# Routed slots with transposed gate and up products, expert weights copied ahead by ScalarE, tables built in the last round, and fillers issued by SyncE and GpSimd

## The reference

```python
logits = hidden @ router_w.T                        # 16 experts
top_vals, top_idx = jax.lax.top_k(logits, 1)
scores = sigmoid(top value at top_idx, -inf elsewhere)
routed_in = hidden[None] * scores.T[:, :, None]
gate, up = split(einsum('nth,nhf->ntf', routed_in, gate_up_proj))   # f = 128 each
routed_out = einsum('ntf,nfh->nth', up * silu(gate), down_proj)
shared = silu(hidden @ shared_gate_w.T) * (hidden @ shared_up_w.T) @ shared_down_w.T
return shared + routed_out.sum(axis=0)
```

## Time and profile before

| | |
|---|---|
| median of 3 runs | 595.18 us (593.46 to 595.81) |
| the profiled execution's own time | 601.01 us |
| its span, first to last instruction | 599.2 us |
| mean granted TensorE clock | 0.941 |
| busy: PE, PEld, DVE, ACT, POOL | 515.9, 408.7, 402.7, 303.2, 348.1 us |
| the 80 stores L1146 | 78.8 us busy, GpSimd idle before them 109.9 us |
| HBM traffic | 21.15 MB read, 17.47 MB written |

### The profile page before, as it was taken

One profiled execution on the slowest core, in us unless ns is written; L12 is line 12 of the kernel. 1 busy time (PEld: TensorE's weight loads), 2 busy tenths in 40 slices (PEclk: granted clock), 3 DMA queues, 4 the chain that ended last, 5 costly groups with the idle time before them and its releaser, 6 DMA issues.

```text
span 599.2 us, 10571 instructions
## 1 busy us (share of the span) xinstructions
PE 515.9 (86%) x2932; PEld 408.7 (68%) x2932; DVE 402.7 (67%) x1113; ACT 303.2 (51%) x539; POOL 348.1 (58%) x542
## 2 busy tenths in 40 slices
PE   1678999999999999999999999985598779797950
PEld 1346777887787887787787789964386668685730
DVE  3769999989998999989997973641134233343423
ACT  3776888678685788678677544211122123122210
POOL 5445587867886787867874764530035453554560
PEclk9888999999999999999999999997799797799985
DMA  5005001101110110110110011126223333333307
GB/s 193 1 1 229 19 15 38 54 11 44 54 45 11 54 36 19 55 36 18 55 36 2 35 36 37 37 91 157 70 62 100 99 96 86 107 94 97 102 11 210
DMA packets 35496, 38.27 MB, mean 64 GB/s; under 512 B 4946, under 2 KB 31706, under 8 KB 35185
## 3 DMA queue, kind: packets, MB, share of 16 engines
q1 hardware_dynamic: 25104, 22.08, 12.3%
q0 software_dynamic: 5632, 12.63, 6.1%
q10 hardware_dynamic: 4704, 2.89, 1.9%
HBM read 21.15 MB, written 17.47 MB: 64 GB/s over the span
## 4 chain that ended last, share of the span: by engine, by line
PE 55%; DVE 11%; issue 11%; another core or an unknown queue 7%; POOL 7%; ACT 6%; ACTq 2%; DMA 1%; POOLq 0%; SPq 0%; DVEq 0%
PE bank L339 13%; PE bank L348 7%; PE bank L332 5%; PE bank L600 5%; DVE an L806 3%; PE bank L326 3%; PE bank L370 2%; PE bank L387 2%; PE bank L410 2%; PE bank L374 2%; PE bank L423 2%; PE bank L403 2%; PE bank L398 2%; PE bank L588 2%
## 5 line engine op out<-in xcount | busy, mean ns | idle before, releaser
L1146 POOL DMA_INDIRECT out<-shared x80 | 78.8, 985 | 109.9 <-DVE shared L1003 90.4
L339 PE MATMUL bank<-hT,wm 128*128 128x256 f32 x512 | 124.7, 388 | 8.9 <-ACT ev L731 7.1
L339 PEld LDWEIGHTS bank<-hT,wm 128*128 128x128 f32 x512 | 95.1, 194 | 28.1 <-issue 8.0
L332 PE MATMUL bank<-wm,k 128*128 128x128 f32 x512 | 63.9, 280 | 2.8 <-ACT k L649 2.8
L332 PEld LDWEIGHTS bank<-wm,k 128*128 128x128 f32 x512 | 62.4, 196 | 4.4 <-ACT k L649 3.6
L751 ACT ACTIVATE num<-bank 128x256 f32<-128x256 f32 x40 | 15.4, 384 | 95.5 <-PE bank L600 45.0
L600 PE MATMUL bank<-wgu,num 128*128 x160 | 49.7, 439 | 4.0 <-ACT num L756 2.9
L1012 DVE TENSOR_TENSOR e<-num,bank 128x256 f32<-128x256 f32 x40 | 16.8, 420 | 53.1 <-ACT num L751 35.9
L806 DVE TENSOR_SCALAR an<-a,mvC,smC 128x128 f32<-128x128 f32 x64 | 43.2, 734 | 1.4 <-POOL smC L1056 1.4
L600 PEld LDWEIGHTS bank<-wgu,num 128*128 128x128 f32 x160 | 31.0, 216 | 10.6 <-issue 6.6
L1135 POOL TENSOR_SCALAR shared<-shared,smA 128x128 f32<-128x128 f32 x64 | 34.7, 549 | 0.2
(11 more groups left out here) (185 smaller groups left out, 1271.8 us busy)
## 6 DMA issues: line engine op xcount, KB each, us to landing
shared<-sorted_rows SPq DMA_DIRECT2D x80, 128.5 KB
shared<-x SPq DMA_DIRECT2D x16, 256.0 KB
wgu<-w_gu SPq DMA_DIRECT2D x1, 2048.0 KB, 8.5
sorted_rows<-filler ACTq DMA_DIRECT2D x10, 128.5 KB, 3.9
out<-shared POOLq DMA_INDIRECT x80
wdn<-w_down SPq DMA_DIRECT2D x1, 1024.0 KB, 10.5
sorted_rows<-rows,posi POOLq DMA_INDIRECT x64
sorted_rows<-filler SPq DMA_DIRECT2D x7, 128.5 KB, 3.2
```

Source lines behind the costliest of these rows:

```text
L332: ins = mm(grp(acc, g), grp(lhs, g), W(name, f), start=(f == 0 and g == 0), stop=(f == F // P - 1), skip_group_check=True)
L339: ins = mm(dst[:, j * HALF:(j + 1) * HALF], W(name, 2 * pair_ + j), src[:, half * HALF:(half + 1) * HALF], start=True, stop=True)
L1146: g_.indirect_dma_start(out, bass.IndirectOffsetOnAxis(xr[k % RING][:, j, 2 * D:ROW].bitcast(U32), 0), xr[k % RING][:, j, D:2 * D], None, ...
```

## The change

**Slots.** Gate and up are computed with the features on partitions: the weights are stationary and the tokens move (4 matmuls of 128 columns instead of 2 of 256 for a pair). The result of silu times up is then already what the down product wants, so the transpose L594, its bank and the copy L1008 are gone, and a pair takes three turns instead of four. The expert's weights are picked by ScalarE: it reads the expert words into its own registers and copies the 256 columns of `wgu` of each slot into `xw` (two buffers, in the place of `q`) a turn ahead. `XT6_B` and `XGU_B` have two banks each. TensorE's order inside a turn is turned round: input transpose, gate and up, down, late steps.

**Tables.** The table steps, now 15 (`tail_p` is new, the free rows plus the partition number), are called in DVE's round code right behind the last update of `region`. The two table matmuls stand ahead of the down product of the last C tile, inside the rounds. PACK is 5, so there are 16 expert words.

**Fillers.** SP issues ten, and GpSimd six as indirect stores behind its last round. ScalarE issues none.

**Late units.** `BEFORE_SLOTS` is 5: unit 5 runs inside the slots, where 28 steps now are spread over the turns. TensorE reads the expert words between steps 1 and 2 of unit 3 instead of behind unit 5.

A few waits on TensorE in the rounds change places with their neighbours (the same waits ahead of the same matmul).

```diff
-PACK = 4
+PACK = 5
...
+        xw = q
...
-        XT6_B, XT7_B, XGU_B, XDN_B = bank[6], bank[7], bank[4], bank[5]
+        XT6_B, XGU_B, XDN_B = [bank[6], bank[1]], [bank[4], bank[7]], bank[5]
...
-        TAB_ROWS = 14
-        SP_FILLS = 6
+        TAB_ROWS = 15
+        SP_FILLS = 10
-        BEFORE_SLOTS = FIRST_LATE + 3
-        TURNS = NP + 3
+        BEFORE_SLOTS = FIRST_LATE + 2
+        TURNS = NP + 2
...
+        def w_of(k, j, part):
+            return xw[k % 2][:, j * 2 * EF + part * EF:j * 2 * EF + (part + 1) * EF]
...
 # SyncE
-            fill_tails(sp, SP_ENGINE, 0, SP_FILLS)
+            sp.wait_ge(s["tab"], 1)
+            for row in entries(SP_ENGINE, tail_i, 0, FILL_ROW - P, SP_FILLS):
+                sp.dma_start(sorted_ap[bass.ds(row, P), :], filler[:, :]).then_inc(s["fill_out"], 16)
...
-            sp.wait_ge(s["fill_out"], 16 * (NE + 1))
+            sp.wait_ge(s["fill_out"], 16 * (SP_FILLS + 1))
+            sp.wait_ge(s["fill_p"], 16 * (NE - SP_FILLS))
...
 # TensorE
+            def table_rows():
+                pe.wait_ge(s["tab"], TAB_ROWS)
+                mm(TAB[0:1, 0:P], rowm[:, :], ident[:, :], start=True, stop=True)
+                mm(TAB[0:1, P:P + WORDS], eidc[:, :], place[:, :], start=True, stop=True).then_inc(s["tab_mm"], 1)
...
                 for t in at(5, C_TILES):
+                    if t == C_TILES[-1]:
+                        table_rows()
                     wait(pe, "cac0", t)
...
             late_step(FIRST_LATE, 1)
-            pe.wait_ge(s["tab"], TAB_ROWS)
-            (the two matmuls)
+            pe.wait_ge(s["tab"], TAB_ROWS + 2)
+            words = list(entries(PE_ENGINE, eid_i, 0, NE ** PACK - 1, WORDS))
             late_step(FIRST_LATE, 2)
...
             def one_turn(m):
+                for k in pair(m, 0):
+                    pe.wait_ge(s[f"xr_in{k % RING}"], 32 * (k // RING + 1))
+                    wait(pe, "xhT", k - 2)
+                    for j in range(2):
+                        ins = nc.tensor.transpose(grp(XT6_B[k % 2], j), xr[k % RING][:, j, 0:D], ident[:, :])
+                    ins.then_inc(s["xT6"], 1)
+                for k in pair(m, 1):
+                    wait(pe, "xhT", k)
+                    wait(pe, "xact", k - 2)
+                    for j in range(2):
+                        wait(pe, "xw", k, j + 1)
+                        mm(grp(XGU_B[k % 2], j), w_of(k, j, 0), grp(xhT[k % 2], j), start=True, stop=True)
+                        ins = mm(grp(XGU_B[k % 2], 2 + j), w_of(k, j, 1), grp(xhT[k % 2], j), start=True, stop=True)
+                    ins.then_inc(s["xGU"], 1)
+                for k in pair(m, 2):
+                    wait(pe, "xact", k)
+                    wait(pe, "xy", k - 1)
+                    (down as before, from xact)
...
 # ScalarE
-            fill_tails(act_e, ACT_ENGINE, SP_FILLS, NE)
+            act_e.wait_ge(s["tab"], TAB_ROWS + 2)
+            words = list(entries(ACT_ENGINE, eid_i, 0, NE ** PACK - 1, WORDS))
+            act_e.wait_ge(s["w_in3"], 32)
...
             def one_turn(m):
+                for k in pair(m, 0):
+                    wait(act_e, "xGU", k - 2)
+                    for j in range(2):
+                        af(xw[k % 2][:, j * 2 * EF:(j + 1) * 2 * EF],
+                           wgu[:, bass.ds(expert_of(words, 2 * k + j) * (2 * EF), 2 * EF)], ACT.Copy).then_inc(s["xw"], 1)
+                    wait(act_e, "xT6", k)
+                    af(xhT[k % 2][:, :], XT6_B[k % 2][:, 0:2 * P], ACT.Copy).then_inc(s["xhT"], 1)
                 for k in pair(m, 1):
                     wait(act_e, "xGU", k)
                     wait(act_e, "xact", k - 2)
+                    af(xsg[k % 2][:, :], XGU_B[k % 2][:, 0:2 * P], ACT.Silu).then_inc(s["xsg"], 1)
...
 # VectorE
                     v.tensor_tensor(region[:, :], TOT, region[:, :], ALU.add).then_inc(s["reg"], 1)
+                    if t == NT - 1:
+                        tables()
...
-                for k in pair(m, 2):
-                    wait(dve, "xT7", k)
-                    wait(dve, "xDN", k - 2)
-                    v.tensor_copy(xaT[k % 2][:, :], XT7_B[:, 0:2 * P]).then_inc(s["xaT"], 1)
...
 # GpSimd
             for n in range(ROUNDS):
                 one_round(n)
+            gp.wait_ge(s["const_d"], 4)
+            gp.wait_ge(s["tab"], 2)
+            for e_ in range(SP_FILLS, NE):
+                g_.indirect_dma_start(sorted_ap, bass.IndirectOffsetOnAxis(tail_p[:, e_:e_ + 1].bitcast(U32), 0), filler[:, :], None).then_inc(
+                    s["fill_p"], 16)
```

More of the change, by code:

```diff
@@ L264, in add_late, with expert_of @@
             eng.wait_ge(s["tl_out"], 16 * N_LATE)
-        def fill_tails(eng, engine, first, last):
-            eng.wait_ge(s["const_d"], 4)
-            eng.wait_ge(s["tab"], 1)
-            for row in entries(engine, tail_i, first, FILL_ROW - P, last - first):
-                eng.dma_start(sorted_ap[bass.ds(row, P), :], filler[:, :]).then_inc(s["fill_out"], 16)
+        def expert_of(words, slot):
+            return (words[slot // PACK] >> (slot % PACK * 4)) & (NE - 1)
+        def w_of(k, j, part):
+            return xw[k % 2][:, j * 2 * EF + part * EF:j * 2 * EF + (part + 1) * EF]
         @block.sync
@@ L586, in one_turn @@
                     wait(pe, "xy", k - 1)
                     for j in range(2):
[L588 removed]
+                        ins = mm(grp(XDN_B, j), grp(xact[k % 2], j), wdn[:, bass.ds(expert_of(words, 2 * k + j) * D, D)], start=True, stop=True)
                     ins.then_inc(s["xDN"], 1)
[L590 to L595 removed]
```

105 lines of the change are left out of this document (36 added, 69 removed).

## The result

| | before | after |
|---|---|---|
| median of the runs side by side | 595.32 us (593.46 to 595.81) | 578.73 us (577.51 to 579.57) |
| ratio after to before, 95% interval | | 0.9718 (0.968 to 0.9757) |
| span of the profiled execution | 599.2 us | 575.7 us |
| first transpose of the slots | 428.77 us | 421.35 us |
| first store, end of the last | 439.68, 584.7 us | 427.22, 560.72 us |

577 us was forecast and 578.73 came: 16.6 us less than before. The two profiled spans differ by 23.5 us, 6.9 more than the medians. The profiled execution of the kernel before was a long one (601.01 us against a median of 595.32) and that of the kernel after a short one (577.51 against 578.73), so parts read from these two traces add up to more than the change is worth.

What follows compares the result with a forecast made beforehand. Change-over and slots were the question, the slots bound by GpSimd's stores coming in runs, holds and restarts. First store 9.7 us earlier plus 9 us in the slots: 19 us off the 599.2 us span, 580.5, times 0.993, 577 us; range 570 to 583.

Steps and rivals of the forecast that it cites:

- hold: Behind a GpSimd run of more than about three stores, TensorE's completion signals arrive late, one 4.5 us late.
- Tables: Change-over: table steps moved ahead of unit 2's products delay TensorE's down group, +2.8 us on its path.
- Fillers: Change-over: taking ten fillers off ScalarE removes TensorE's idle 7.12 us, -7.1 us.
- Registers: Change-over: TensorE reads 16 expert words in place of 20, -1.4 us.
- The sum of the start: First slot transpose moves from 428.8 to 417.2 us, or 422.6 with a hold; 421 taken, gain 7.8 us.
- The first store: Start of slots: about 9 us behind the first transpose, before 10.9; it moves from 439.7 to 430, 9.7 us.
- The slots: Restart behind a hold falls from 7.6 to 5.2 us, in six 3.40 us stretches; 9 us taken, bounds 0 and 20.
- rival C: Slots: runs of four stores with 3.2 us of hold behind each, turn 4.2 us; slower, 608 us; chance 0.12.
- The criteria: Wrong if outside waits of silu or weight copies grow over 32 us, or stores stretch over 140 us.
- A: Only the start gains, 9.7 us; holds set the slots' rate whatever feeds GpSimd; 585.5 us; chance 0.20.
- B: No holds at the start, weak ones in slots: first store 13.7 us earlier, slots 20 shorter; 562 us; chance 0.18.
- D: No gain: start gains only 6.2 us and the late unit moved into the slots costs 5.2; 594 us; chance 0.08.

Runs made afterwards that it cites:

- e6: Changed kernel with one small GpSimd instruction as a pause behind every store: 574.01 us, ratio 0.9583.
- e5: Changed kernel with two small GpSimd instructions as pauses behind each pair of stores: 585.8 us, ratio 0.9768.
- e8: Changed kernel with all 16 fillers issued by SP and one small GpSimd instruction behind every store: 570.09 us, ratio 0.9591.
- e10_tables_behind_rounds: Changed kernel with the table steps back behind the rounds and the table matmuls behind unit 3's second product: 577.27 us, ratio 0.9702.
- e3_start_of_before: Changed kernel with the change-over of the kernel before, new slots kept: 586.86 us, ratio 0.9861.
- e2_slots_of_before: Changed kernel with the slots of the kernel before, new change-over kept: 588.04 us, ratio 0.9872.
- e11: Changed kernel with stores of 16 of 128 columns sent to another array, routed results left out: 576.83 us, one run, no ratio.
- e12: Changed kernel with a GpSimd pause behind every store and one ahead of each of its six fillers: 563.37 us, ratio 0.9908.

## Why the prediction was right

**How near, and how much of it is luck.** The mechanism was right in its main part, as below, but 577 against 578.73 is nearer than the sum deserves. By the two profiled executions the sum was too small: 19 us off the span were forecast (9.7 + 9) and 23.5 came (12.5 + 11.5, less 0.5 at the tail, which is 15.0 us in place of 14.5). The step from span to median then went the other way: the prediction took the median as 0.993 of the span, and after it is 1.005 (578.73/575.7), 7 us more. The two misses nearly cancel. Side by side the medians differ by 16.6 us, where 595.18 - 577 = 18 was forecast.

**What bounds the kernel.** The hold is real. With the density taken out of GpSimd's runs, and more work for it, the kernel is faster, 0.9591 against 0.9700 with SP's fillers on one chip (and 0.9583 in e6 against 0.9718, across chips), and all or most of the waits without a sender are gone in e5 and e8. The Trainium skill's rule that completion signals cost 26 ns each ("TensorE: Matmul & The Clock Gate", The cost: per-tile semaphore tail) doesn't cover this: in the rows above a signal is 2.7 us late behind GpSimd's run, and in e5_rest_pair2 no wait is without a sender, with the same products.

**Tables.** Charged with +2.8 us on TensorE's path; L353 starts at 394.23 in place of 392.15, so 2.1 (2.5 behind the last region). As e10_tables_behind_rounds shows, it doesn't reach the end of the chain while the hold is there, so it stood in the sum for nothing.

**Fillers.** The 7.12 us are gone, as forecast, and back in e3_start_of_before (7.64). SP's ten were taken at 0.5 us each, from 396 to 402; they took 9.29 us, from 395.0 to 404.3. The first load was put at 407.4 "or a little later" and came at 408.90.

**Registers.** -1.4 us: from the start of the load to the next product it was 428.77 - 421.3 = 7.5 us and is 412.26 - 406.2 = 6.1 (the load begins at 406.2 in the view of that source line). Right.

**The sum of the start.** 417.2 without a hold and 422.6 with one, 421 taken, 421.35 measured. The hold costs 3.0 us and not 5.4, and without it the start would be at 418.4 and not 417.2. A term of that size was missing: behind the read of the words unit 3's down product runs at the low clock and takes 3.50 us, where the same 16 passes take 2.16 at 419.36 with the clock at 1.00. Inside the run a signal is late by 1.9 us; signals don't all wait for its end. The 421 was a choice between two sums, with no row for what lies between them, and it fell well by luck.

**The first store.** "With one stage less, about 9" us behind the first transpose: it is 5.9 (427.22 - 421.35). This is the term that was most off, 1.9 us expected and 5.0 measured. The 10.9 us of before were not four equal stages, and they ran at a clock of 0.67, which the prediction didn't look at here. With the old slots behind the new start, at a clock of 1.00, it is 8.6 us (e2_slots_of_before), with the new slots behind the old start, at 0.63, 7.0 (e3_start_of_before). Both count: the stage less, and the register read moved away from the first transpose. The low clock behind it isn't gone by that; it now lengthens what stands ahead of the first transpose. So 12.5 us came and not 9.7.

**The slots.** 9 us taken, 11.5 measured, 10.4 with the old start, and 7.8 against the old slots behind the new start (141.3 - 133.5). Copies taken at 0.40 us are 0.412. The mechanism was right in its main part: what shrank is what follows a hold. The count was wrong: the prediction had six stretches of the kind of 3.40 us, and before there are three (3.40, 3.40 and 3.41, at 477.75, 501.77 and 525.24 us), which at 2.4 us each is 7 us and not 14. They are gone altogether. The rest came from a place where the sum had nothing: the stretch at the hold itself, 3.24 us in the earlier trace rows, is 2.1. Most of that difference is that now the add itself is held: the store follows the held instruction by 1.2 us (460.47, 461.69), where before it followed the held silu by 2.0 (470.11, 472.08). Where 16 stretches made 45.6 us, 14 make 31.2. GpSimd's idle time beyond the 0.3 us between stores is 133.5 - 103.2 = 30.3 us, where 33 were forecast. But the shape that came is the one of rival C: runs of four with a stretch behind each. The prediction put that stretch at 3.2 us, and with it a turn at 4.2 us; it is 2.1, and a turn 3.5, under the 3.87 from which C decides. Had the 14 stretches been 3.2 us long, as C had them, 14 x 1.1 = 15 us of the 16.6 would have been lost again, so the forecast was near its other side.

**The criteria.** The silu's waits without a sender fell to 11.9 us, under the 32 that would have shown the prediction wrong, but the same kind of wait appeared at DVE's add, which the criterion didn't name, with 54.7 us. A criterion on a signal has to name all who may wait for it.

**Rivals.** A is refuted by e3_start_of_before. B needed a chip or a kernel without holds; the pauses come to it (566.8 us of span in e8_all_sp_rest, where B had 565.5). D fell with the stage: it had the stores 5.2 us longer, and they are 11.5 shorter; its start (422.6) was only 1.2 us off.

## What to carry to other kernels

A busy engine that issues indirect DMAs back to back can hold up signals of engines that have nothing to do with it. One sees it where a consumer starts long after its producer's end and a microsecond behind the end of such a run, with no sender in the profile. If so, test it by making the issuing engine slower: here a pause of 0.3 us behind every store takes 25 us of GpSimd's time and brings the ratio from 0.9700 to 0.9591 on one chip, some 6.5 us. And measure on more than one chip before keeping such a pause: if one has no holds, only the price of the pause is left there, and much of what a change seemed to gain may be a shorter wait behind a hold.

## What the runs showed that was not expected

- One chip ran the kernel before in 568.70 us, two others in 595.32 and 597.95, with nearly the same granted clock (0.955 to 0.958 there, 0.935 to 0.956 elsewhere).
- The start differs between chips too: with the same fillers from GpSimd the first transpose is 33.4 to 33.5 us behind the last region in the four kernels of one chip, and 30.9 to 31.6 in after, e2, e10 and e11.
- On one chip a step of 1.43 us between GpSimd's indirect writes leaves 56.4 us of waits without a sender and one of 1.56 us leaves 6.9; on another chip 1.56 us leaves 47.8.
- SP's ten filler issues took 9.29 us beside GpSimd's dense fillers (0.93 each), sixteen took 8.57 us with no filler of GpSimd (0.54 each), and ten took 5.51 us beside GpSimd's fillers with pauses (on the chip of e12). GpSimd's run seems to slow SP's issue too.
- A 256-column copy in SBUF costs ScalarE 0.412 us, an evacuation of as many columns from PSUM 0.38 (L757).
